# Gate rows of experts 1 to 7 by DMA from one partition, in place of broadcast turns on TensorE

## The reference, cut to what matters

```python
p = softmax(h @ Wg)                    # (B, S, 8)
gate = top-2 of p, normed to sum 1     # (B, S, 8), 0 for experts not chosen
y = 0
for n in range(8):
    u = relu(h @ W1[n] + b1[n])        # (B, S, 256)
    y += gate[:, :, n] * (u @ W2[n] + b2[n])
```

## Time and profile before

| what | us |
|---|---|
| median of 3 runs | 2255.79 |
| lowest and highest run | 2252.53, 2262.1 |
| profiled execution, its time | 2253.47 |
| its span in the profile | 2251.7 |
| busy in it: PE, DVE, ACT, POOL | 2038.6, 1808.6, 1586.6, 1163.2 |

### The profile page before, as it was taken

One profiled execution on the slowest core, in us unless ns is written; L12 is line 12 of the kernel. 1 busy time (PEld: TensorE's weight loads), 2 busy tenths in 40 slices (PEclk: granted clock), 3 DMA queues, 4 the chain that ended last, 5 costly groups with the idle time before them and its releaser, 6 DMA issues.

```text
span 2251.7 us, 82659 instructions
## 1 busy us (share of the span) xinstructions
PE 2038.6 (91%) x34492; PEld 1475.1 (66%) x34492; DVE 1808.6 (80%) x3751; ACT 1586.6 (70%) x3041; POOL 1163.2 (52%) x1413
## 2 busy tenths in 40 slices
PE   6888899987679999999999999999999999999996
PEld 4666664445457776777777777777767777767773
DVE  6778775467578898898988888888888888888883
ACT  4666753355467778777878778778787777877773
POOL 1111110000177667666766767666676766667660
PEclk9999999999789999999999999999999999999998
DMA  4000000000122223232232223222232322322220
GB/s 111 1 2 2 2 1 1 0 1 1 47 56 75 57 70 89 70 82 60 73 92 73 68 59 103 66 76 64 66 94 68 85 61 65 99 68 72 59 75 20
DMA packets 94676, 125.83 MB, mean 56 GB/s; under 512 B 27484, under 2 KB 42466, under 8 KB 94306
## 3 DMA queue, kind: packets, MB, share of 16 engines
q1 hardware_dynamic: 94306, 120.54, 20.5%
HBM read 21.91 MB, written 1.05 MB: 10 GB/s over the span
## 4 chain that ended last, share of the span: by engine, by line
PE 59%; DVE 10%; ACT 5%; issue 4%; POOL 1%; POOLq 0%; ACTq 0%; DVEq 0%
PE oo L557 17%; PE pj L557 15%; PE tr L560 13%; PE sc L557 11%; ACT arena L1761 3%; PE tr L557 2%; DVE arena L1593 2%; DVE xn L1212 2%; DVE arena L1614 1%; DVE arena L1616 1%; DVE arena L1595 1%; PE oo L560 1%; ACT sc L1761 1%; ACT xcur L1761 1%; DVE arena L1601 1%
## 5 line engine op out<-in xcount | busy, mean ns | idle before, releaser
L2139 POOL TENSOR_TENSOR arena<-arena 128x1024 f32<-128x1024 f32 x192 | 457.0, 2380 | 332.4 <-DVE arena L1595 332.4
L1761 ACT ACTIVATE arena<-tr 128x512 f32<-128x512 f32 (+2 forms) x874 | 461.6, 571 | 157.9 <-PE tr L560 109.8
L1761 ACT ACTIVATE arena<-pj 128x512 f32<-128x512 f32 x576 | 341.4, 598 | 188.4 <-PE pj L557 149.2
L560 PE MATMUL tr<-ident,arena 128*128 128x128 f32 x2974 | 429.1, 279 | 19.0 <-DMA beta<-in_L_attn_betas 10.1
L560 PEld LDWEIGHTS tr<-ident,arena 128*128 128x128 f32 x2974 | 341.8, 142 | 105.9 <-issue 52.8
L1761 ACT ACTIVATE arena<-arena 128x16 f32<-128x16 f32 (+6 forms) x808 | 354.4, 452 | 56.1 <-DVE arena L1380 27.7
L2157 POOL TENSOR_TENSOR arena<-arena 128x1024 f32<-128x1024 f32 x192 | 365.5, 1904 | 23.2 <-POOL arena L2150 0.9
L1593 DVE TENSOR_TENSOR arena<-pj,rtab 128x512 f32<-128x512 f32 x384 | 259.8, 677 | 30.0 <-ACT arena L1761 27.1
L557 PE MATMUL oo<-slab,arena 64*32 64x64 f32 (+1 forms) x12416 | 231.1, 228 | 37.9 <-issue 23.3
L1595 DVE TENSOR_TENSOR arena<-pj,rtab 128x512 f32<-128x512 f32 x384 | 261.5, 681 | 0.0
L1601 DVE TENSOR_REDUCE arena<-arena 128x8 f32<-128x512 f32 x384 | 255.4, 677 | 0.0
(11 more groups left out here) (273 smaller groups left out, 3832.3 us busy)
## 6 DMA issues: line engine op xcount, KB each, us to landing
slab<-arena SPq DMA_DIRECT2D x576, 128.0 KB, 2.4
slab<-arena SPq DMA_DIRECT2D x336, 64.0 KB, 2.0
wqkv<-in_L_ffn_Wqkv SPq DMA_DIRECT2D x18, 512.0 KB, 4.3
wo<-in_L_ffn_Wo SPq DMA_DIRECT2D x6, 512.0 KB, 4.3
w<-in_L_ffn_W SPq DMA_DIRECT2D x6, 341.0 KB
YT<-in_L_attn_x SPq DMA_DIRECT2D x4, 256.0 KB, 3.7
arena<-in_L_ffn_W SPq DMA_DIRECT2D x1, 1024.0 KB
out_x<-arena SPq DMA_DIRECT2D x4, 256.0 KB, 2.2
```

The lines of the kernel that those rows point to most:

```text
L560: return nc.tensor.transpose(o, i, ident[0:i.shape[0], 0:i.shape[0]])
L1761: return nc.scalar.activation(o, i, f, **k)
L2139: p_.tensor_tensor(r_, r_, rb[:, k, :], ALU.add).then_inc(sum_ok, 1)
```

## The change

For experts 1 to 7 TensorE's `spread` is left out. In its place SyncE issues seven DMAs a batch once `sT` is written; each copies one partition's row of 512 gates (2 KB) to all 128 partitions of a buffer `gate_rows`, which lies over the attention buffer `PTh`, free in this stage, with two sets for even and odd batches. VectorE waits for the DMA of its expert (`gate_in[n]`) and reads the gates from there. Expert 0 is done as before.

```diff
+        gate_rows = PTh.rearrange("p a b c -> p (a b c)")[:, 0:2 * (NE - 1) * S].rearrange(
+            "p (k n s) -> p k n s", k=2, s=S)
...
+        gate_in = [sem(f"gate_in{n}") for n in range(NE)]
...
+            def gate_spread(b):
+
+                sp.wait_ge(s_ev, b + 1)
+                if b == 0:
+                    sp.wait_ge(pv_done, B * H0 // 4)
+                if b >= 2:
+                    sp.wait_ge(m_sc, (b - 1) * NE)
+                for n in range(1, NE):
+                    sp.dma_start(gate_rows[:, b % 2, n - 1, :], sT[n:n + 1, :].unsqueeze(1).broadcast_to([1, P, S])
+                                 ).then_inc(gate_in[n], 16)
+
+            for b in range(B):
+                gate_spread(b)
             sp.wait_ge(scores, B * (H0 + H1) * T)
...
             def spread(j):
                 b, n = divmod(j, NE)
+                if n > 0:
+                    return
...
                     ve.wait_ge(m_relu, j * 2 + 2)
-                    ve.wait_ge(m_bc, j + 1)
+                    if n == 0:
+                        ve.wait_ge(m_bc, b + 1)
+                        gate = tr[:, j % 2]
+                    else:
+                        ve.wait_ge(gate_in[n], b * 16 + 16)
+                        gate = gate_rows[:, b % 2, n - 1, :]
                     if j >= 2:
                         ve.wait_ge(m_y, j - 1)
-                    v.tensor_tensor(hsc[:, j % 2], hes[:, j % 2],
-                                    tr[:, j % 2].unsqueeze(1).broadcast_to([P, 2, S]),
+                    v.tensor_tensor(hsc[:, j % 2], hes[:, j % 2], gate.unsqueeze(1).broadcast_to([P, 2, S]),
                                     ALU.mult).then_inc(m_sc, 1)
```

## The result

The changed kernel takes 2388.4 us (median of 4 runs, 2379.3 to 2390.4) where the kernel before takes 2254.4 us (4 runs): a ratio of 1.058, 95% interval 1.055 to 1.061. That is 134 us slower.

A forecast was written before the change was run, and what follows sets the result against it. TensorE sets the pace before, the gates after. Four batches of 75.6 us less 3.4 make 299.0, against 156.1 before: +142.9; +3 for the clock gives 2399.4 profiled, with the median 2.3 above: 2402 us, range 2345 to 2458.

The forecast's parts named there:

- The bound moves to the gates: In the expert stage, a row every 10.0 us against expert slots of about 4.2 us makes multiplies of experts 1 to 7 wait.
- The row time: Time for one copy of a row from one partition to 128: taken as 10.0 us, range 8.2 to 12 us.
- one DMA engine's worth of reads: Assumed rate of reads from one partition: 418 / 16 = 26.1 GB/s, from the loads' 418 GB/s on 16 DMA engines.
- The estimate of 2388 us: Total time if one port gives the skill's 27.6 GB/s, with a row in an estimated 9.5 us.
- The sum of a batch: Expert stage, per batch: 2.2 + 7 x 10.0 = 72.2 us to the last row, then 3.4 us, 75.6 us in all.
- the turn: Between batches, from the multiply of expert 7 to the end of the next copy of `sT`: 3.4 us.
- The 3 us for the clock behind the stage: Last `down` and start of the second layer, about 3 us of matmul on the path, run slower: +3 us.
- The saving of 7 us: Expert stage: gain from the spreads removed from TensorE if the gates came for nothing, with 12.3 us as its bound.
- 16 spreads on the path: Of 28 removed spreads of 0.44 us, those not covered by waits or avoided by batch 3's chain: 7 us.
- Landing of the copies: Issue-to-landing time of a batch's seven copies: grows with their place, median about 40 us.
- The rival of fast copies: In the expert stage, copies at 0.63 us a row hide behind slots of about 4 us: 2249 us, chance 11%.

The follow-up runs named there:

- one_door: two_doors with ScalarE's four copies reading partitions 0 to 3, so that both streams read from partitions 0 to 3: 2420.3 us in one run.
- two_doors: The changed kernel with rows 1 to 3 still issued by SyncE and rows 4 to 7 issued by ScalarE: 2359.7 us in one run.
- order_alt: The changed kernel with its copies issued on the one queue in the order 1, 4, 2, 5, 3, 6, 7: 2327.7 us in one run.
- no_copies: The changed kernel without gate copies; multiplies of experts 1 to 7 read a constant block of weights without waiting: 2253.1 us, ratio 0.9990 to the kernel before.
- by_hbm: The changed kernel with the 8 rows first stored to HBM and the seven copies reading from there: 2253.1 us, ratio 0.9979 to the kernel before.
- wide_source: The changed kernel with each of the 28 copies reading 128 partitions of a block of weights: 2252.8 us, ratio 0.9981 to the kernel before.
- two_rows: The changed kernel with only experts 3 and 6 getting gates by the narrow copy, the others keeping `spread`: 2256.3 us, ratio 0.9986 to the kernel before.

## Why the prediction was right

The time of 2388.4 us lies in the range of 2345 to 2458, 13.6 us below the point of 2402.

- *The bound moves to the gates.* Right: the multiplies of experts 1 to 7 wait in steps of one row, the DMA share is near full at 27 GB/s, and the next batch does not start early.
- *The row time,* the open price, was taken as 10.0 us from 418 / 16 = 26.1 GB/s. It measured 9.7 us, 27 GB/s. The reason given with it, one DMA engine's worth of reads, was a number near the right one and not the cause: the prediction said that it came out the same whether reads queue at the partition or run on one engine. So the nearness of the number is in part luck. The strips show all 16 engines busy, and one_door against two_doors and order_alt put the limit at the source's door. This is what the Trainium skill says (SBUF — State Buffer, "Door 1: The DMA port swizzle"), with 27.6 GB/s for one port, the door of this text; the runs agree for these reads, at 27 GB/s, with partitions 0 to 3 behind one and 4 to 7 behind another. The estimate of 2388 us that the prediction worked out from that figure was nearer than its sum.
- *The sum of a batch* was 75.6 us and measured 71.9. Per row 0.3 us less makes 2.1 of it. Row 7 came sooner than a full step, 7.6 us after row 6 in batches 0 and 1 (379.49 to 387.11 in the first), about 2 us; our reading is that no later copy takes a share of the door from it, which no run tests. Against that the turn was 0.5 us longer, for the lower clock.
- *The 3 us for the clock behind the stage* did not come: from 603 to 613 us the granted clock is 1.00, as from 475 to 485 us before.

```profile
603.00:613.00 10.00, 9.68 (x26) 4.30 (x25) 8.49 (x14) 4.92 (x8) 0.00 (x0) 1.00 0.01 2
```

```profile
475.00:485.00 10.00, 10.00 (x27) 4.47 (x26) 8.71 (x14) 4.92 (x8) 0.00 (x0) 1.00 0.01 2
```

In the stage itself TensorE was expected to be busy for under half of the time, with 0.61 as the clock of such a stretch; it was busy for 63% (181.26 of 287 us), its matmuls being slower, at 0.81. From the last multiply to the end the profiled executions take 1776.7 us before, 1785.2 with the change, but also 1784.3 in no_copies and 1780.8 in by_hbm, where TensorE is never starved. The execution varies by more than the term. The errors partly cancel: against the sum the stage is 14.7 us shorter and the part behind it 5.6 longer, which makes 9 us in the profiled execution; the rest of the 13.6 is that this execution (2390.4 us) lies 2.0 above the median of the runs, where the sum took it to lie 2.3 below.
- *The saving of 7 us* by 16 spreads on the path came out at 5.0 us in the stage of no_copies. The count was right: batches 0 to 2, where all 16 stand, gave 6.8 us. What it left out is the clock: batch 3 lost 1.8 us, with a granted clock of 0.83 where it had been 1.00. That TensorE, with less to do in it, lost its full clock for this reason is our reading; the dip stands in each of the profiled executions of no_copies, wide_source, by_hbm and two_rows, and not in the one of the kernel before. In the changed kernel all this is hidden.
- *Landing of the copies.* I forecast a median of about 40 us, growing with their place. It was 31.1, the time of 3.2 rows, since SyncE is held in its issues: the chain of the changed kernel has SyncE in its issues, each time one row long.

```profile
391.50 0.60 SPq L538
...
392.14 6.89 SPq L538
...
399.08 9.74 SPq L538
```

The third issue of a batch takes 6.9 us and the fourth 9.7. A copy is issued later, so its own landing time stops growing. Our reading is that only some three copies have room at once; what sets the limit is not shown.

The rival of fast copies priced the result without the narrow source at 2249 us, and the runs with a wide source or HBM are at about 2253, beside 2257.5 of the kernel before.

## What to carry to other kernels

Before a broadcast is moved to DMA, look at where its bytes are read, not only at how many there are: 128 reads of one partition run at 27 GB/s, a row of 2 KB to all partitions takes 9.7 us, and the 16 DMA engines look busy all the while. Compare that with the slot in which the row is needed: two rows in eight slots of 4 us, through two doors, are free, seven are the new bound. If many rows must go, a bounce through HBM has the first of them in place 4.9 us after the copy of `sT` (317.22 to 322.10 in by_hbm), where the narrow copy took 12. It removes the loss, but gains next to nothing on the kernel before: 0.2%, where two_rows has 0.1%. Work taken off the busiest engine is worth only what isn't already covered by another engine's wait, less what the clock takes back: here 12.3 us of work gave 6.8 on the path, and 5.0 after a dip of the clock.

## What the runs showed of the hardware

- A DMA issue can hold its engine when earlier copies are slow: up to 9.7 us an issue on SyncE, 21 to 28 us for four on ScalarE with two doors and 25 to 41 with one, but at most 2.4 us for four on GpSimd. On a computing engine this delays what stands behind it.
- Two streams through two doors exceed one door's 27 GB/s, with slices up to 57, but over a batch they did not reach the sum; of the kernels that read both doors at once, one run each, the best was one queue with doors in turn (2328 us), the worst a stream on GpSimd beside one on SyncE (2396 us).
- With 28 of 32 spreads gone and no wait for gates (no_copies), TensorE's granted clock fell to 0.83 for some 10 us of the stage, and one `up` took 3.51 us in place of 1.88.
- HBM serves 128 reads of one 2 KB row without such a limit: slices of 3.9 us of by_hbm show up to 326 GB/s.
